# A five-stage cross-attention chain: where the row maxima, their subtraction and the last MLP tiles stand in the order of work

## The reference

```
x0: cross attention, mask per sequence  -> + MLP (256 -> 1024 -> 256, exact gelu)     stage 0
x1: cross attention                                                                  stage 1
x2: self attention, padding mask        -> + MLP                                     stage 2
x3: self attention, causal, in halves                                                stage 3
x4: cross attention                     -> + MLP                                     stage 4
x5: cross attention, 16 heads of 64, RMS norm                                        the tail
head:   out = softmax(mask(q k^T)) v,   16 heads of 16 channels in stages 0 to 4
block:  x = x + out w_o + b;   MLP: x = x + gelu(ln(x) w1 + b1) w2 + b2
```

## Time and profile before

| | |
|---|---|
| three runs | 5414.97 us (5398.02 to 5416.44) |
| the profiled execution, its own time | 5400.48 us |
| its span | 5398.7 us |
| mean granted TensorE clock | 0.965 |
| busy: TensorE, VectorE, ScalarE, GpSimd | 88%, 49%, 42%, 17% |

### The profile page before, as it was taken

One profiled execution on the slowest core, in us unless ns is written; L12 is line 12 of the kernel. 1 busy time (PEld: TensorE's weight loads), 2 busy tenths in 40 slices (PEclk: granted clock), 3 DMA queues, 4 the chain that ended last, 5 costly groups with the idle time before them and its releaser, 6 DMA issues.

```text
span 5398.7 us, 69019 instructions
## 1 busy us (share of the span) xinstructions
PE 4766.1 (88%) x25220; PEld 1891.7 (35%) x25220; DVE 2635.8 (49%) x5280; ACT 2287.3 (42%) x2869; POOL 919.6 (17%) x831
## 2 busy tenths in 40 slices
PE   5888888888888888888899988888885999999999
PEld 2333333333233333333444433333332333333333
DVE  5544445446666444444345565454431555545554
ACT  3444444445554434434444444444431433333332
POOL 0111111101110101101011111111000433333333
PEclk8999999999999999999999999999997999999999
DMA  1111111111111000001021121111101000000000
GB/s 56 36 38 45 36 46 43 38 60 61 62 67 49 33 29 34 29 28 37 29 74 57 57 71 40 49 42 34 34 28 67 1 12 12 12 12 1 12 12 9
DMA packets 152296, 201.67 MB, mean 37 GB/s; under 512 B 18993, under 2 KB 102321, under 8 KB 150706
## 3 DMA queue, kind: packets, MB, share of 16 engines
q1 hardware_dynamic: 151986, 197.31, 10.7%
HBM read 128.86 MB, written 68.42 MB: 37 GB/s over the span
## 4 chain that ended last, share of the span: by engine, by line
PE 70%; DVE 14%; issue 9%; ACT 5%; DMA 1%; DVEq 0%; SPq 0%; ACTq 0%; POOL 0%; POOLq 0%
PE psT L604 9%; PE small L554 7%; PE psT L680 7%; PE psT L688 7%; PE psO L625 6%; PE small L561 6%; PE psS L582 6%; PE psT L814 4%; DVE nmb L1043 4%; PE psT L610 3%; DVE out L1040 3%; ACT probs L871 3%; PE psT L554 2%; PE psT L779 2%; PE psO L829 2%
## 5 line engine op out<-in xcount | busy, mean ns | idle before, releaser
L871 ACT ACTIVATE probs<-psT 128x1024 f32<-128x1024 f32 (+3 forms) x1280 | 1158.9, 958 | 1206.0 <-PE psT L610 560.8
L1043 DVE TENSOR_REDUCE nmb<-psS 128x2 bf16<-128x1024 f32 (+3 forms) x768 | 839.3, 1093 | 675.4 <-PE psS L582 412.5
L604 PE MATMUL psT<-low 32*128 32x512 f32 (+3 forms) x5120 | 740.1, 621 | 149.5 <-DVE xe L1102 59.1
L582 PE MATMUL psS<-out 32*128 32x512 bf16 (+3 forms) x2560 | 484.9, 375 | 279.7 <-DVE nmb L1043 139.3
L1040 DVE CUSTOM_DVE_ANT_0 out<-psS,pens_sb 128x512 f32<-128x512 f32 x1024 | 665.8, 687 | 111.9 <-issue 84.7
L625 PE MATMUL psO<-probs,V 128*32 128x512 f32 (+3 forms) x5120 | 657.3, 586 | 1.0 <-ACT probs L871 1.0
L1209 DVE TENSOR_REDUCE parts<-psS 128x2 bf16<-128x1024 f32 x256 | 314.9, 1230 | 522.5 <-PE psS L801 522.5
L582 PEld LDWEIGHTS psS<-out 32*128 32x128 bf16 x2560 | 120.8, 91 | 1056.5 <-DVE nmb L1043 456.4
L981 ACT ACTIVATE probs<-psT 128x1024 f32<-128x1024 f32 x256 | 262.2, 1024 | 526.0 <-PE psT L817 526.0
L680 PE MATMUL psT<-out,W 128*128 128x512 f32 x768 | 387.4, 631 | 22.2 <-ACT out L893 22.2
L688 PE MATMUL psT<-W,gel 128*128 128x256 f32 x1536 | 378.4, 391 | 0.8 <-ACT gel L916 0.8
(11 more groups left out here) (152 smaller groups left out, 5077.2 us busy)
## 6 DMA issues: line engine op xcount, KB each, us to landing
o_mid<-out SPq DMA_DIRECT2D x160, 256.0 KB, 2.0
oN<-o_mid SPq DMA_DIRECT2D x160, 128.0 KB
oN<-r_mid SPq DMA_DIRECT2D x80, 256.0 KB
x_mid<-xe SPq DMA_DIRECT2D x40, 512.0 KB, 2.9
xw<-x_mid SPq DMA_DIRECT2D x36, 512.0 KB, 4.1
xe<-x_mid SPq DMA_DIRECT2D x36, 512.0 KB, 4.8
cT<-ctxT SPq DMA_DIRECT2D x20, 512.0 KB, 3.7
W<-wm SPq DMA_DIRECT2D x6, 1024.0 KB, 7.6
```

The source lines that it names most:

```text
L582: last = nc.tensor.matmul(psS[e][:, 0:n], Qb[rows_of(j), q, a, c, qt * P:(qt + 1) * P], Kb[rows_of(j), q, c, 0:n], start=True, stop=u.s != ...
L604: last = nc.tensor.matmul(psT[j][:, q0:S], Kf[rows_of(j), q, a, c, kt * P:(kt + 1) * P], Qf[rows_of(j), q, a, c, q0:S], start=True, stop=p ...
L871: nc.scalar.activation(probs[:, i % 2, two, q0:S], psT_all[:, two, q0:S], ACT.Exp, scale=float(DH) ** -0.5)\
L1043: nc.vector.tensor_reduce(nmb4[:, g % 2, qt, row:row + 33:32], psS_both[:, :, 0:n], AX, ALU.max)\
```

## The change

- In an MLP body the last two of the four MLP output tiles go to the bank `small` (a new use `z` at slot 19.5); the first two share one bank of `psT`. VectorE reads the first bank after the thirteenth pair of the block, the second after the sixteenth. exp_scores of step 10 waits only for the first reading; the next fill of `small` (`q1`) waits for the second.
- The first matmul of the block waits only for `h0`, the second for `h1`.
- `LEADS`: an MLP body now finds 24 of its 32 pairs done, and does the other eight one per step, in steps 1 to 8, ahead of exp_scores. If the next body is an MLP body too, it does pairs 16 to 23 of `nxt` in steps 12 to 15, two per step. The first body of stages 0, 2 and 4 does these eight pairs in its steps 8 to 11 (one more each, behind the fills) and 14 and 15 (two more each). The other bodies keep 16 and two pairs per step.
- Pair 16 of `nxt`, the first that reads the second half of the queries and keys, waits for `k1` to be read.
- `m2` moves from slot 15 to 11 (MLP bodies) or 10 (others); in MLP bodies `m0` moves from slot 27 to 22 and `v1` from 29 to 27.
- The second pair of a step now stands behind outputs only where the step's odd slot holds a q, k, v, y or w; before, wherever it held anything.
- The mask conversion moves from slot 15 to 17 in MLP bodies.

```diff
-CUR_USES = {True: {"m1": 1, "m2": 15, "m3": 17}, False: {"m1": 1, "m2": 15, "m3": 21}}
+CUR_USES = {True: {"m1": 1, "m2": 11, "m3": 17}, False: {"m1": 1, "m2": 10, "m3": 21}}
-MLP_USES = {"h0": 18, "h1": 19}
+MLP_USES = {"h0": 18, "h1": 19, "z": 19.5}
-NXT_USES = {True: {"x0": 7, "x1": 8, "q0": 9, "k0": 16, "q1": 21, "k1": 23, "v0": 25, "m0": 27, "v1": 29},
+NXT_USES = {True: {"x0": 7, "x1": 8, "q0": 9, "k0": 16, "q1": 21, "m0": 22, "k1": 23, "v0": 25, "v1": 27},
-MASKS_AT = 15
+MASKS_AT = {True: 17, False: 15}
+LEADS = {True: 24, False: 16}
+IN_BLOCK = 16
+def maxima_plan(mlp, out):
+    if mlp:
+        last = (1, 1, 0) if out > IN_BLOCK else (0, 0, 0)
+        return [(0, 0, 0)] + 8 * [(1, 0, 0)] + 3 * [(0, 0, 0)] + 4 * [last]
+    if out > LEADS[False]:
+        return 8 * [(1, 1, 0)] + 4 * [(1, 1, 1)] + 2 * [(1, 1, 0)] + 2 * [(1, 2, 1)]
+    return 16 * [(1, 1, 0)]
...
@@ max_scores
-                        pe.wait_ge(small_read, place.fills("nxt", "k0") + 2)
+                        pe.wait_ge(small_read, place.fills("nxt", f"k{c}") + 2)
@@ hidden
+                    if m == 0:
+                        pe.wait_ge(small_read, place.fills("prev", f"h{c}") + 2)
@@ from_hidden
+                dst = psT[2] if t < 2 else small[:]
...
@@ body of TensorE: (before, beside, after) are the three numbers of the plan
+                for i, (before, beside, after) in enumerate(place.body.maxima()):
                     late = place.body.at(2 * i + 1)
+                    long = any(use[0] in "qkvyw" for _, use in late)
+                    after_mlp = place.body.mlp and i == MLP_AFTER + 1
+                    maxima(before)
                     if cur is not None:
+                        if after_mlp:
+                            pe.wait_ge(sem["z_read"], count("z_read", prev, 1))
                         exp_scores(place, cur, i)
                     for owner, use in place.body.at(2 * i):
                         fill(place, owner, use, prev, cur, nxt)
+                    if not long:
+                        maxima(beside)
...
+                    if i > 0 and cur is not None and not after_mlp:
                         outputs(cur, i - 1)
+                    if long:
+                        maxima(beside)
                     for owner, use in late:
                         fill(place, owner, use, prev, cur, nxt)
+                    maxima(after)
                     if place.body.mlp and i == MLP_AFTER:
                         mlp(place, prev, cur, nxt)
...
@@ VectorE
+            def mlp(place, u, nxt):
+                for n in range(IN_BLOCK):
+                    if nxt is not None:
+                        maximum(nxt, n // 2, n % 2)
+                    if n == 3 * IN_BLOCK // 4:
+                        take_hidden(place, u, 0)
+                take_hidden(place, u, 1)
```

More of the change, by code:

```diff
@@ L97, in __init__, with maxima @@
             found += [(k, "nxt", u) for u, k in COUNT_USES.items()]
+        self.out = LEADS[False]
         self.uses = sorted(found, key=lambda f: f[0])
         self.order = {(who, u): i for i, (_, who, u) in enumerate(self.uses)}
+    def maxima(self):
+        n, steps = LEADS[self.mlp] if self.cur is not None else 2 * STEPS, []
+        for i, counts in enumerate(maxima_plan(self.mlp, self.out)):
+            if self.cur is None and i < STEPS // 2:
+                steps.append(([], [], []))
+                continue
+            step = []
+            for k in counts:
+                pairs = range(n, n + k)
+                n += k
+                step.append([divmod(at, 2 * STEPS) for at in pairs if at < 2 * STEPS or self.nxt is not None])
+            steps.append(tuple(step))
+            if self.mlp and i == MLP_AFTER:
+                n += IN_BLOCK
+        return steps
     def at(self, slot):
@@ L158, in schedule, with with_leads @@
     return out
-SCHEDULE = schedule()
+def with_leads(parts):
+    bodies = [body for _, part in parts for body, *_ in part]
+    for body, after in zip(bodies, bodies[1:]):
+        body.out = LEADS[after.mlp]
+    return parts
+SCHEDULE = with_leads(schedule())
 FILLS = sum(len(body.uses) * max(turns, 1) for turns, bodies in SCHEDULE for body, *_ in bodies)
@@ L440, in store @@
                 dst = tokens(at_row(x_mid, u))
[L441 to L444, removed]
+                sp.wait_ge(small_read, place.fills("prev", "z" if u.s in MLP else "y1") + 2)
                 sp.dma_start(dst, xe[:]).then_inc(sem["x_out"], 16)
@@ L702, in mlp @@
                 for m in range(FC):
-                    hidden(u, m)
+                    hidden(place, u, m)
                     maximum_next(m)
@@ L1144, in between, with maxima @@
                         normalise(1, xe, xn, halves(1)).then_inc(sem["normed_m"], 1)
-            def body(place, prev, cur, nxt):
[L1147 to L1155, removed]
-                        take(place, who, use, prev, cur, nxt)
-                    if mlp and slot == 2 * MLP_AFTER + 1:
-                        if nxt is not None:
-                            for m in range(FC):
-                                maximum(nxt, m, 0)
-                                maximum(nxt, m, 1)
-                        take_hidden(prev)
+            def mlp(place, u, nxt):
[5 more added lines that the diff above has]
+                take_hidden(place, u, 1)
+            def body(place, prev, cur, nxt):
+                units = (cur, nxt)
+                def maxima(pairs):
+                    for ahead, n in pairs:
+                        maximum(units[ahead], n // 2, n % 2)
+                for i, (before, beside, after) in enumerate(place.body.maxima()):
+                    maxima(before)
+                    between(place, 2 * i, prev, nxt)
+                    for who, use in place.body.at(2 * i):
+                        take(place, who, use, prev, cur, nxt)
+                    maxima(beside)
+                    between(place, 2 * i + 1, prev, nxt)
+                    for who, use in place.body.at(2 * i + 1):
+                        take(place, who, use, prev, cur, nxt)
+                    maxima(after)
+                    if place.body.mlp and i == MLP_AFTER:
+                        mlp(place, prev, nxt)
             nc.vector.memset(V[:], 1.0)
```

50 lines of the change are left out of this document (23 added, 27 removed).

## The result

The changed kernel takes 5274.62 us, median of four runs (5257.99 to 5290.06), beside 5411.27 for the kernel before on the same chip: a ratio of 0.975, 95% interval 0.9731 to 0.977. It is faster by 2.5%, 137 us. 5295 was forecast, in a range of 5225 to 5375. The profiled execution is the fastest of the four: 5257.99 us, span 5256.2, against 5400.48 and 5398.7, so the two profiles stand 142.5 us apart.

A forecast was written before the change was run, and what follows sets the result against it. TensorE was busy 88% of the span, with 282 us of gaps in eighteen MLP bodies. Terms -155, +49 and -9 gave -115 on 5400.5, so 5285.5; half the 14.5 us to the median made 5295, range 5225 to 5375.

The forecast's parts named there:

- steps 0-3: Start of MLP loop bodies: one pair instead of two leaves ScalarE's chain as limit; 4.2 us saved masked, 3.55 plain.
- step 4: MLP loop bodies: still waits for ScalarE to read `x1` ahead of `q0`; stays at 6.4 us masked, plain 0.2 less.
- steps 5-8: MLP loop bodies: fewer pairs and `m2` moved out of a wait; 4.2 us saved masked, 3.55 plain.
- step 9, block: MLP block: gaps at both ends go, 0.9 us at its begin and 2.7 at its end; saves 4.3 masked, 3.45 plain.
- step 10: Behind the MLP block: ScalarE's table reload, 1.28 us, is late next; saves 0.85 us masked, 0.65 plain.
- step 11: MLP loop bodies: pair 16 waits about 2.04 us for `k1` ahead of exp_scores; costs 2.7 us masked, 3.0 plain.
- steps 12-14, clock: End of loop bodies: added pairs cost 1.9 us masked, 1.75 plain; half clock behind the wait another 1.3 per body.
- first bodies: First bodies of stages 0, 2 and 4: eight pairs more cost 16.5, 17.5 and 15.5 us, together +49.
- other fourteen: Bodies of stages 1 and 3: `m2` leaves a step where exp_scores waited; -0.5 us each.
- 0.7 and 2.7: Two masked bodies with less half clock to lose: -5.7 us each, -11 together, before the clock charge.
- Step 7: MLP loop bodies: loses a pair, `m2` and the wait for it; 5.9 us becomes 3.75 to 4.0, 2.0 saved.
- rival B: Half the gain, 5355 us: `y0`'s chain of transfers comes next and step 5 gives back the early gain; chance 0.12.

The follow-up runs named there:

- `m2` alone: Kernel before with one edit, `m2` at slot 11 (MLP bodies) and 10 (others) instead of 15: 5364.94 us, 0.9917.
- Block alone: Kernel before with only the last two MLP tiles in `small`, first hidden tile split by halves, additions placed as in the change: 5296.84 us, 0.9775.
- outputs first at `x`: Kernel with 16 pairs ahead everywhere, its second pair moved behind outputs where a step's fill is `x0` or `x1`: 5199.77 us, 0.9601.
- no-leads kernel: Changed kernel with 16 pairs ahead everywhere, MLP bodies two pairs per step in steps 0 to 7 and none at the end: 5208.84 us, 0.9615.
- `y0` later: Changed kernel with `y0` filled behind outputs of step 5 and `m2` ahead of them in MLP bodies: 5262.72 us, 0.9709.

## Why the prediction was right, and which terms were off

The total stands: 115 us forecast in the profiled pair, 142.5 measured; 5295 forecast, 5274.62 measured. By parts, us per body, forecast and measured:

```
                        masked x12        plain x6
steps 0-3             -4.2   -4.1      -3.55  -2.0
step 4                 0      0        -0.2   -0.2
steps 5-8             -4.2   -4.9      -3.55  -1.3
step 9, block         -4.3   -4.9      -3.45  -3.8
step 10               -0.85  -0.7      -0.65  -0.5
step 11               +2.7   +2.6      +3.0   +2.8
steps 12-14, clock    +3.2   +2.5      +3.05  +1.35
step 15                 -    -0.15       -    +0.4
body                  -7.7   -9.6      -5.35  -3.35
first bodies x3 +16.5 forecast, +15.1 measured; other fourteen -0.5, -1.0
in sum: 0.7 and 2.7 -9, -13; 1.0 and 3.0 -18, -15.5; 4.7 and the last -4, -9
```

The total is nearer than its parts. Masked bodies gained 23 us more than forecast and the other rows some 16 us more; the plain ones gained 12 us less.

1. *Steps 0 to 3, masked: right.* One pair per step leaves ScalarE's chain as the limit, 3.75 to 3.9 us per step.
2. *Block and step 10: right in mechanism, too small in size* by 0.5 us per masked body and 0.2 per plain one. The addition is hidden as claimed, the table's reload is what is late next. That exp_scores cover the second addition was wrong: `q1` waits for it, 12.4 us in 20 places.
3. *Step 7: right in size, partly wrong in cause.* I gave the 2.0 us to the pair, `m2` and the wait together; `m2` alone brings 2.1.
4. *Step 11, the new wait: right.* 51.8 us in 24 places for 47 in 23; the price of the whole wait was shown by moving one pair. The Trainium skill's rule that matmuls run strictly in order (TensorE: Matmul & The Clock Gate, Part 3) fits: exp_scores waited behind the pair in the one kernel and ran in its place in the other.
5. *Clock behind it: right on average in masked bodies, and nothing in plain ones.* Half clock began in step 12 of 8 of the 12 masked bodies and in the wait itself in a ninth (2.2). In these nine step 12 took 6.9 us instead of 5.3, 1.2 us per masked body on average for my 1.3. It began there in none of the plain ones, so their 8 us were charged for nothing. Elsewhere clock was gained that I had counted only as the missing gap: half clock began in step 10 of 19 bodies before and of one (4.7) after.
6. *Plain bodies: the term that failed.* Steps 0 to 3 and 5 to 8 gain 3.3 us instead of 7.1. Two causes. In step 5 `y0` waits for GpSimd, as rival B said, 13.4 us in the six bodies, and step 5 grew by 1.75 on average. In the trace of the kernel before, GpSimd's scaling ends 0.8 to 1.9 us before `y0` starts in plain loop bodies. This margin of about 1 us was smaller than the 3.55 that steps 0 to 3 were to gain, so my own numbers said that B happens in plain bodies; I had weighed it as a rival for all eighteen. In masked bodies the margin was 2.5 to 3.4 us and not my 4, and 0.1 to 1.2 us of it are left: B was near there too. Moving `y0` took back 1.95 us of that step. The other is step 0, which grew from 4.06 to 4.61 through bodies 4.3 and 4.5 (7.09 and 7.60 us, 3.25 in the other four). Both open a new turn of the loop. TensorE is idle there for 2.4 us before exp_scores and for 1.5 and 1.8 us in their midst, and no semaphore ended either. In the kernel before it was idle in the same two bodies for 1.9 and 2.0 us, ahead of the first pair. What it does in that time stays open.
7. *First bodies: right*, +17.9 in steps 8 to 15 where I had +17.5, +16.5 and +15.5, less 2.7 in the steps before these.

**What the prediction did not ask.** Its sum is by steps, and by steps it hides that the change holds an edit that loses. Put together by edit, from its own terms, the leads gain 4.2 x 12 + 3.55 x 6 = 72 in steps 0 to 3 and (0.55 + 0.85) x 18 = 25 in steps 5 and 6. They pay 4.6 x 12 + 4.75 x 6 = 84 in steps 11 to 14, less 6 for `m0`, 26 for clock and 49 in the first bodies: 153 against 97, a loss of 56. Bodies 0.7, 1.0, 2.7 and 3.0, counted in the same way, give some 13 back, which leaves a loss of about 43. Measured, taking them out brings 66 us by the medians. Block alone brings 122 and `m2` alone 54, 176 in sum, where all but the leads brings 210 (5418.71 less 5208.84); the other 34 were not separated. The order of second pair and outputs and the places of `m0`, `v1` and the mask conversion, which those two kernels leave as before, may be the source, or the two parts bring more together than singly; no run tells these apart.

The two fastest kernels are those without leads and with outputs first at `x`: 5199.77 and 5199.58 us, 0.960 and 0.959 of before, 75 us under the changed kernel's median. They were not timed against it in one comparison.

## What to carry to other kernels

Sum a change twice, by place and by edit: work moved from full steps into later ones is a gain only if the later ones have room on the engine that it moves to, and here all of the gain in steps 0 to 3 came back in steps 11 to 15, with the first bodies' cost on top. An operation with a wait belongs behind the work that does not need it, in an engine that issues in order. Before shortening the steps ahead of a chain of transfers, compare the chain's slack with what they are to lose, in each kind of body separately.

## What the runs showed of the hardware

- The granted clock fell in or just behind an idle piece of 2.1 or 2.3 us before step 12 in 9 of 12 masked bodies. The same pieces in the other three, and one of 2.2 us in each of the six plain bodies, were followed by full clock. So the length of the piece alone does not decide it; what does, these runs do not show.
- In body 1.3 TensorE was idle for 2.92 us in steps 2 and 3 of the no-leads kernel (0.78, 0.34 and 1.80), and the clock fell. With outputs first it was idle for 2.82 us in the same steps (0.94, 0.34, 0.81, 0.32 and 0.41), and it did not. The sums are nearly alike; the longest piece differs.
- Half clock also lengthens the fills that engines wait for. `y0` in body 4.1 took 2.96 us instead of 1.99 and ended that much later for VectorE, so that the step with a wait of 3.31 us took 9.46 us, 3.9 more than the 5.52 of before.
- From the issue of the load of the reciprocals to GpSimd's start it was 5.7 us in 4.1 of the changed kernel and 5.5 with `y0` later. With the scaling (2.34 us) `y0` could start 8.2 us after the issue, which in the changed kernel came only 3.6 us before step 5 began.
